# The rows of maxima issued from ScalarE's queue instead of SyncE's, in a kernel of two attentions and two feed-forwards

## The reference

```
x = x + attention_a(layernorm(x))   # 16 heads of 8, biases, two masked score columns
x = x + ffn(layernorm(x))           # top 2 of 8 experts for an item, from its mean token
x = x + attention_b(layernorm(x))   # 16 heads of 8, no biases
x = x + ffn(layernorm(x))
```

## Time and profile before

| | us |
|---|---|
| median of 3 runs | 1102.5 |
| lowest and highest | 1100.66, 1109.38 |
| the profiled execution | 1098.47 |
| its span in the trace | 1096.7 |
| TensorE, VectorE, ScalarE, GpSimd busy | 911.2, 788.5, 759.2, 594.6 |
| mean granted clock of TensorE | 0.961 |

### The profile page before, as it was taken

One profiled execution on the slowest core, in us unless ns is written; L12 is line 12 of the kernel. 1 busy time (PEld: TensorE's weight loads), 2 busy tenths in 40 slices (PEclk: granted clock), 3 DMA queues, 4 the chain that ended last, 5 costly groups with the idle time before them and its releaser, 6 DMA issues. The chain is left out here.

```text
span 1096.7 us, 27550 instructions
## 1 busy us (share of the span) xinstructions
PE 911.2 (83%) x10204; PEld 527.5 (48%) x10204; DVE 788.5 (72%) x1398; ACT 759.2 (69%) x1324; POOL 594.6 (54%) x1011
## 2 busy tenths in 40 slices
PE   1468999999998898884876899899998899988667
PEld 1234555555555455442753455555555555544356
DVE  0467888888888788852447788888878888887144
ACT  1147777878877777783753678777777787777556
POOL 4555566666666566332355466666656666652311
PEclk9889999999999999997996999999999999999879
DMA  8544444444444544300034444444444444441013
GB/s 230 157 137 137 137 138 137 137 138 137 138 137 137 136 139 135 111 3 20 1 111 131 128 139 139 137 137 137 138 137 137 137 138 137 138 137 43 1 49 107
DMA packets 140516, 131.64 MB, mean 120 GB/s; under 512 B 9880, under 2 KB 121888, under 8 KB 140256
## 3 DMA queue, kind: packets, MB, share of 16 engines
q1 hardware_dynamic: 139312, 128.49, 40.7%
q10 hardware_dynamic: 1072, 1.40, 0.5%
HBM read 73.75 MB, written 55.57 MB: 118 GB/s over the span
## 5 line engine op out<-in xcount | busy, mean ns | idle before, releaser
L379 DVE TENSOR_REDUCE nmax<-ring 128x4 f32<-128x1024 f32 x512 | 606.5, 1217 | 132.2 <-PE ring L504 130.6
L418 ACT ACTIVATE probs<-ring 128x1024 f32<-128x1024 f32 x512 | 510.4, 1027 | 115.9 <-PE ring L521 112.7
L504 PE MATMUL ring<-k_stack,q_stack 64*128 64x256 bf16 x2048 | 202.9, 278 | 105.5 <-DMA k_stack<-scratch 84.6
L486 PE MATMUL values_bank<-probs,values 128*32 128x256 f32 x4096 | 275.6, 387 | 5.8 <-ACT probs L418 5.8
L335 POOL TENSOR_SCALAR xy<-x,mv,rstd 128x128 f32<-128x128 f32 x256 | 201.2, 795 | 8.7
L521 PE MATMUL ring<-q_stack,k_stack 64*128 64x256 bf16 x2048 | 188.2, 273 | 0.8 <-DVE nmax L379 0.6
L504 PEld LDWEIGHTS ring<-k_stack,q_stack 64*128 64x128 bf16 x2048 | 82.6, 96 | 192.1 <-ACT probs L418 97.5
L298 POOL TENSOR_SCALAR mparts<-nmax 128x32 bf16<-128x32 f32 x64 | 13.8, 216 | 263.4 <-DVE nmax L379 263.4
L486 PEld LDWEIGHTS values_bank<-probs,values 128*32 128x32 f32 x4096 | 107.1, 109 | 90.8 <-issue 24.1
L521 PEld LDWEIGHTS ring<-q_stack,k_stack 64*128 64x128 bf16 x2048 | 84.4, 94 | 75.1 <-issue 36.8
L450 ACT COPY values<-m_bank 128x128 f32<-128x128 f32 x128 | 28.9, 278 | 81.2 <-PE m_bank L565 81.2
(11 more groups left out here) (99 smaller groups left out, 1039.4 us busy)
## 6 DMA issues: line engine op xcount, KB each, us to landing
q_stack<-scratch SPq DMA_DIRECT2D x128, 256.0 KB
k_stack<-scratch SPq DMA_DIRECT2D x128, 256.0 KB
scratch<-parts SPq DMA_DIRECT2D x128, 192.0 KB, 3.6
scratch<-parts SPq DMA_DIRECT2D x128, 128.0 KB, 5.3
scratch<-parts SPq DMA_DIRECT2D x128, 64.0 KB, 4.3
out<-x SPq DMA_DIRECT2D x32, 128.0 KB, 1.8
q_stack<-maxT SPq DMA_DIRECT2D x128, 12.0 KB
scratch<-in_tail SPq DMA_DIRECT2D x8, 128.0 KB, 3.5
```

The lines of the kernel that those rows point to most:

```text
L379: nc.vector.tensor_reduce(dst, src, axis=AX.X, op=ALU.max, negate=True).then_inc(max_done, 1)
L418: nc.scalar.activation(probs[g % 2][:, c:c + 2, :, :], pair_of_exps(n, p)[:, :, :].rearrange("p x (k q) -> p x k q", k=TILES), ACT.Exp).th ...
L486: last = nc.tensor.matmul(values_bank[32 * c:32 * (c + 1), a * TOKENS:(a + 1) * TOKENS], values[item % RING][:, k, PER_GROUP * g + c, :], ...
L504: last = nc.tensor.matmul(pair_of_scores(n, p)[:, a, t * TOKENS:(t + 1) * TOKENS], q_stack[z][rows, p, t * P:(t + 1) * P], k_stack[z][rows ...
```

## The change

SyncE no longer waits for the copy to `maxT`, and no longer issues the two DMAs of the rows of maxima. ScalarE issues them, right behind its copy: it waits for the copy's own semaphore and for all eight max-side scores of item n+1, then issues both, and goes on to `oT` and exp 1. SyncE's queue carries only loads and bounces. Sizes, buffers, and what waits for the DMAs stay as they are.

```
--- before.py
+++ after.py
@@ -258,12 +258,6 @@
                 sp.wait_ge(tail_in, 4 * 16 if masked else 2 * 4 * 16)
 
                 def step(n, r, live, half):
-                    if live(1):
-
-                        sp.wait_ge(maxT_ready, (n + 1) + 1)
-                        for par in range(2):
-                            dst = q_stack[(r + 1) % RING][BLOCK * par + MAX_ROW:BLOCK * par + MAX_ROW + 3, :, :]
-                            sp.dma_start(dst, maxT[(r + 1) % 2][3 * PAIRS * par:3 * PAIRS * (par + 1), :]).then_inc(max_in[(r + 1) % 2], 16)
                     if live(3):
 
                         D = scratch[0 if masked else 1][(r + 3) % 2]
@@ -424,6 +418,11 @@
                                 act.wait_ge(max_in[(r - 1) % 2], half(-1) * 32 + 32)
                             nc.scalar.copy(maxT[(r + 1) % 2][:, :],
                                            m_bank[:, :].bitcast(BF16)[0:6 * PAIRS, 0:TOKENS]).then_inc(maxT_ready, 1)
+                            act.wait_ge(maxT_ready, (n + 1) + 1)
+                            act.wait_ge(s_done, (n + 1) * PAIRS + PAIRS)
+                            for par in range(2):
+                                dst = q_stack[(r + 1) % RING][BLOCK * par + MAX_ROW:BLOCK * par + MAX_ROW + 3, :, :]
+                                act.dma_start(dst, maxT[(r + 1) % 2][3 * PAIRS * par:3 * PAIRS * (par + 1), :]).then_inc(max_in[(r + 1) % 2], 16)
                         if p == 0 and live(-1):
                             act.wait_ge(pv_done, (n - 1) * GROUPS + GROUPS)
                             nc.scalar.copy(oT[(r - 1) % 2][:, :, :], values_bank[:, :].rearrange("p (a q) -> p a q", a=SHARES)).then_inc(oT_ready, 1)
```

## The result

The changed kernel takes 1114.3 us (median of 12 runs, 1110.2 to 1118.5), the kernel before 1102.2 (12 runs, 1095.8 to 1109.4). The ratio is 1.0105, with a 95% interval of 1.0076 to 1.0134: slower by 12 us, where 44 were forecast. The profiled execution took 1114.6 us, its span is 1112.8.

The account below looks back on a forecast made before the run. No engine was taken as full: a closed loop through SyncE's wait and issues made loads late. Losing 96 us on ScalarE and gaining 52 gave +44 on the 1102.5 median, forecast 1147 us, own range 1128 to 1162.

Parts of the forecast that it names:

- The loop and its opening: SyncE's wait for the maxima copy and its issues make loads late; removing them gains 52 us.
- the M0 wait: TensorE's wait for loads at a step's first scores, 56.1 us in all; claimed to go, gaining 49 us.
- Nothing new is late: At TensorE's M1 and transposes: exp 7 (0.42 us after line 592) and GpSimd's last split (0.73) both fit.
- ScalarE's pair: Two issues between ScalarE's copy and `oT` delay exp 1 and M3 by 1.55 us, in 62 steps 96 us.
- behind M3 TensorE has no slack: After the fourth scores TensorE is practically full for 9.00 us, so added idle time cannot be won back.
- The sum: Whole kernel: 96 us lost on ScalarE less 52 us gained on the loads, +44 us.
- They block: ScalarE's issues hold up what is queued behind them: `oT`, exp 1, then the `qk` copy; 1.58 us a pair.
- If ScalarE works on while it issues: Sign that the prediction is wrong: ScalarE not standing still during its DMA issues; no size given.
- Cheap issues: Rival: ScalarE's pair costs less than 0.87 us, so the change gains; at 0.28 each, 1085 us; chance 0.11.
- Collision: Rival: ScalarE's issues wait for SyncE's loads, up to 1.2 us a step, 1184 to 1221 us; chance 0.11.
- The loads not earlier: Rival: bounces or queue are the real limit, so 96 us come without the 52, 1198 us; chance 0.03.
- the band of up to 1120: Rival's upper part: somewhat more than 1% slower if part of the delay is absorbed behind M3; chance 0.04.

Follow-up runs that it names:

- sp_after_loads: Kernel before, with SyncE keeping the wait for the copy and the two issues, but behind its four loads: 1040.1 us, ratio 0.9467.
- wait_loads_issues: Kernel before, SyncE still waiting for the copy ahead of its loads, but the two issues moved behind them: 1039.5 us, ratio 0.9539.
- sp_four: Kernel before, with each of SyncE's two issues cut into halves, so four issues ahead of its loads: 1187.1 us, ratio 1.0897.
- act_and_gate: Changed kernel, with SyncE's wait for the copy of the maxima put back ahead of its loads, without the issues: 1113.8 us, ratio 1.0146.
- one_each: Changed kernel, but ScalarE issues only one of the pair behind its copy, SyncE the other behind its loads: 1066.1 us, ratio 0.9709.
- act_late: Changed kernel, with ScalarE's pair of issues placed behind exp 3 in the program instead of behind the copy: 1037.8 us, ratio 0.9458.
- act_after_oT: Changed kernel, with ScalarE's pair one instruction later, behind the `oT` copy: 1105.8 us, ratio 1.0151.
- act_after_exp1: Changed kernel, with ScalarE's pair behind exp 1, ahead of the `qk` copies: 1059.2 us, ratio 0.9606.
- act_four: Changed kernel, with each of ScalarE's two issues cut into halves, four issues with the same bytes: 1295.2 us, ratio 1.1882.
- act_oT_done: Changed kernel, with ScalarE's pair behind the `oT` copy and a wait until that copy has ended: 1150.2 us, ratio 1.0443.

## Why the prediction was right in direction and wrong in size

**The loop and its opening: right.** That the loads were late because of what stood ahead of them in SyncE's program, that the bounces were there early enough, and that the M0 wait would go, is shown by sp_after_loads, wait_loads_issues and sp_four. I gave 52 us for it; on one chip it is 57 (1097.4 - 1040.1). A part of the difference is the 0.14 us that I left standing behind line 592 at each M0; in the second attention M0 starts 0.06 us before that matmul's end.

**Nothing new is late: wrong, and it mattered.** I wrote of the exp 7 that M1 needs and of GpSimd's last split, which the transposes need, that "both fit". Neither does. The exp comes at 0.42 us behind line 592, and M0 can now start at -0.06, so M1 stands 0.54 us behind M0 (700.38, 700.92 in the changed kernel) where it stood 0.43 behind. The split ends 0.75 us behind line 592 in sp_after_loads, and the transposes start 0.11 us after that. They stand behind M1 in the program, but behind a weight load that had to wait, like M1's, the next group comes 0.33 us later elsewhere in the step (706.54, 706.87); here it is 0.38 (709.38, 709.76). So the split is the last to arrive, by an estimated 0.05 us. The values matmuls follow, and `oT` waits for those: they stand 1.16 us behind M0, where it was 0.98 before. No run moved the exp or the split alone, so this division is read from rows and not tested; that `oT` waits 0.31 us is in the trace.

**ScalarE's pair, the term that failed: 1.55 us a step forecast, 1.14 and 1.23 measured (step lengths of the change less those of sp_after_loads).** The mechanism was right, the size wasn't: I let nothing hide the pair but the 0.14 us that `oT` waited in the step as it was. Of the second attention's 0.32 us of error, 0.17 are the cover (0.31 instead of 0.14, the step above), 0.11 the pair (1.47 instead of 1.58, SyncE's price taken for ScalarE's), 0.04 the time around it (0.07 instead of 0.11). In the first attention `oT` stands 0.28 us behind the copy in sp_after_loads and 1.56 in the changed kernel, which would make 12.93 + 1.28 = 14.21 and not 14.07; 0.14 us are won back behind M3: the transposes of `oT` wait for the second of two `qk` activations, 0.35 us in sp_after_loads, 0.21 in the changed kernel. I had written that behind M3 TensorE has no slack. In all 31 x 1.14 + 31 x 1.23 = 73 us instead of 96, and act_and_gate less sp_after_loads, on one chip, is 1113.8 - 1040.1 = 74.

**The sum.** Two large terms of opposite sign left a small rest: 96 - 52 = 44 was forecast, 1113.8 - 1097.4 = 16 comes from one chip (act_and_gate for the change), 12 is measured over 12 runs of both. An error of a quarter in the pair's term took away half of the forecast (22 of 44), and the 5 us of more gain another tenth. The 4 us between 16 and 12 lie in the kernel before and not in the changed one, which took 1097.4 in one call and 1102.2 in the other.

**They block: half right.** An issue holds up what is behind it, and its price is its length: one_each (0.48 us for one) and the change (1.23 for two) differ by 0.75 in the second attention, which is one issue, and both are about 0.3 less than their issues, which is the cover. But it can lie beside the activations ahead of it (act_late, act_after_oT, act_after_exp1), which the rows at the start of the run couldn't show. "If ScalarE works on while it issues" was among my signs of being wrong; in the change itself it stands still, since the issues wait for the copy just ahead of them.

**The rivals.** Cheap issues: no, 713 ns was the least (its sum, done over with 0.28 us each, makes 0.53 us and not 0.56; nothing hangs on it). The Trainium skill's DMA: Bandwidth & Descriptors ("Issuing engines are not separate DMA queues") calls the sequencer's time usually small beside the transfer. Here the trace of the changed kernel has the pair's packets 4.8 to 6.7 us behind its first issue (medians of 64 for the first and the last packet), and the pair's issues take 1.47 us. Small beside the transfer or not, that time decides: ScalarE's chain waits for the issues, and nobody waits for the transfer. Collision: no; of the lock that Perfetto Trace Analysis of the Trainium skill describes ("DMA Instruction — HWDGE (DVE, Sync)"), act_and_gate shows nothing where both queues start at once. The loads not earlier: no. What came out lies below my own range of 1128 to 1162 and in the band of up to 1120 that I had given a chance of 0.04, from a part of the delay being absorbed. I had put that behind M3 only; in the second attention it is all ahead of M3.

## What to carry to other kernels

An issue of this transfer costs its engine 0.7 us, with 12 KB or with 6 KB; one of the loads, 256 KB each, costs SyncE 0.58 to 0.60. Before you move one, look not for the engine with the lower busy share but for the place in a program behind which nobody waits. The same two issues cost 57 us ahead of SyncE's loads, 74 behind ScalarE's copy, and nothing behind the loads or behind ScalarE's exp 3. When a change is the difference of two large terms, take each cover from the step as it will be, not as it is: what holds up the head of the step now will be gone.

## What the runs showed of the hardware beyond that

An issue on ScalarE starts while the activation ahead of it runs, 0.06 us after its start in act_after_oT, or even before the activation ahead of it has started, by 0.70 us in act_late, and hides there (exp 2 to exp 3 stays 0.92 us). SyncE's and ScalarE's issues run side by side without stretching each other where they started together (0.59 and 1.47 us). In act_four, with a pause of TensorE of 2.4 us in each step, the granted clock of a long window is 0.90, and sixteen matmuls take 1.93 instead of 1.07 us behind the pause. With a pause of 1.70 us (act_oT_done) 6 of 62 steps are longer, by up to 1.6 us, each with a stretch at a granted clock of 0.50.
